# A vision tower with relative attention on one core: the second layer norm's operations dealt out one per head, and four buffers in place of two between the projections and their split

## What is computed

```python
L, H, D, DH, DF = (4, 16, 256, 64, 1024)
h = x                                             # [8, 257, 256]
for i in range(L):
    q, k, val = jnp.split(h @ W_qkv[i], 3, axis=-1)
    q, k, val = (t.reshape(b, s_len, H, DH) for t in (q, k, val))
    kr = (r @ W_r[i]).reshape(s_len, H, DH)
    AC = jnp.einsum('bqhd,bkhd->bhqk', q + u, k)
    BD = jnp.einsum('bqhd,khd->bhqk', q + v, kr)
    prob = jax.nn.softmax((AC + BD) * inv_sqrt_d, axis=-1)
    vec = jnp.einsum('bhqk,bkhd->bqhd', prob, val).reshape(b, s_len, H * DH)
    h = layer_norm(h + vec @ W_o[i], ln1_g[i], ln1_b[i])
    ff = jax.nn.relu(h @ W_ff1[i] + b_ff1[i]) @ W_ff2[i] + b_ff2[i]
    h = layer_norm(ff, ln2_g[i], ln2_b[i])        # the second layer norm
```

## Time and profile before

| what | before |
|---|---|
| median of 3 runs | 2686.0 us (2684.62 to 2693.15) |
| the profiled execution | 2691.76 us, of it 2689.9 us span |
| PE busy | 2219.9 us, 83% of the span |
| DVE busy | 1818.4 us, 68% |
| ACT busy | 1611.9 us, 60% |
| POOL busy | 1186.1 us, 44% |
| head loops (first L1254 of iteration 0 to the last of iteration 31) | 186.6 us to 2349 us of the span, 32 iterations of about 68 us |

### The profile page before, as it was taken

One profiled execution on the slowest core, in us unless ns is written; L12 is line 12 of the kernel. 1 busy time (PEld: TensorE's weight loads), 2 busy tenths in 40 slices (PEclk: granted clock), 3 DMA queues, 4 the chain that ended last, 5 costly groups with the idle time before them and its releaser, 6 DMA issues. The chain is left out here.

```text
span 2689.9 us, 60914 instructions
## 1 busy us (share of the span) xinstructions
PE 2219.9 (83%) x19212; PEld 1640.5 (61%) x19212; DVE 1818.4 (68%) x5490; ACT 1611.9 (60%) x5053; POOL 1186.1 (44%) x2191
## 2 busy tenths in 40 slices
PE   0169989988988988989888898998888999851898
PEld 0146666666666666667666666666666666531565
DVE  8747777777767777777677777776777777625333
ACT  2136666666667666666676666766667667621222
POOL 3025455554555555544565555455655554212011
PEclk9679999999999999999999999999999999975999
DMA  5444333345454333344543333445433333239110
GB/s 166 95 114 105 93 93 93 93 109 140 119 152 103 93 86 93 90 132 125 149 108 93 93 89 93 125 130 142 109 91 91 91 92 90 60 83 311 50 42 26
DMA packets 382056, 285.85 MB, mean 106 GB/s; under 512 B 44711, under 2 KB 350473, under 8 KB 381099
## 3 DMA queue, kind: packets, MB, share of 16 engines
q1 hardware_dynamic: 374603, 262.93, 38.1%
q10 hardware_dynamic: 4864, 12.68, 1.4%
q0 software_dynamic: 2272, 6.35, 0.6%
HBM read 120.84 MB, written 60.48 MB: 67 GB/s over the span
## 5 line engine op out<-in xcount | busy, mean ns | idle before, releaser
L1254 ACT ACTIVATE E<-E,nb 128x257 f32<-128x257 f32 x1024 | 512.8, 508 | 37.1 <-DVE nb L1430 36.9
L975 PE MATMUL bk<-hin,w_sb 128*128 128x257 f16 x3072 | 425.9, 275 | 14.9 <-ACT rel L1192 7.4
L1430 DVE CUSTOM_DVE_ANT_0 E<-bk,cb 128x257 f32<-128x257 f32 x1024 | 390.3, 419 | 64.9 <-PE bk L1068 64.5
L1392 DVE TENSOR_TENSOR pt<-bk,pt 128x512 f16<-128x512 f32 x512 | 354.4, 692 | 64.1 <-ACT pt L1241 55.1
L1023 PE MATMUL bk<-ident,E 128*128 128x128 f32 x2048 | 323.6, 281 | 83.9 <-ACT E L1254 60.5
L975 PEld LDWEIGHTS bk<-hin,w_sb 128*128 128x128 f16 x3072 | 297.1, 98 | 70.0 <-issue 12.6
L1023 PEld LDWEIGHTS bk<-ident,E 128*128 128x128 f32 x2048 | 221.9, 141 | 163.6 <-ACT E L1254 149.8
L1241 ACT ACTIVATE pt<-bk 128x512 f16<-128x512 f32 x512 | 306.4, 598 | 5.8 <-PE bk L1023 5.8
L923 POOL TENSOR_SCALAR wf<-wf 128x256 f32<-128x256 f32 x216 | 93.1, 431 | 434.2 <-DMA wf<-in_w_dram 261.7
L1067 PE MATMUL bk<-kh,qs 128*128 128x257 f16 x1024 | 255.5, 275 | 9.9 <-DMA kl<-rk 9.7
L1068 PE MATMUL bk<-kl,qs 128*128 128x257 f16 x1024 | 255.2, 275 | 0.0
(11 more groups left out here) (277 smaller groups left out, 4409.3 us busy)
## 6 DMA issues: line engine op xcount, KB each, us to landing
qs<-rq SPq DMA_DIRECT2D x256, 128.5 KB, 3.5
kh<-rk SPq DMA_DIRECT2D x256, 128.5 KB, 3.3
kl<-rk SPq DMA_DIRECT2D x256, 128.5 KB, 3.5
wf<-in_w_dram SPq DMA_DIRECT2D x168, 128.0 KB, 2.7
w_split_dram<-wh SPq DMA_DIRECT2D x168, 128.0 KB, 2.2
w_sb<-w_split_dram SPq DMA_DIRECT2D x18, 1024.0 KB, 7.2
wf<-in_we_dram SPq DMA_DIRECT2D x96, 128.0 KB, 2.5
we_split_dram<-wh SPq DMA_DIRECT2D x96, 128.0 KB, 1.8
```

Of the source, the lines that this page charges most:

```text
L975: r = mm(bank[4 + s % 2][:, 0:S], wcol(a, C_QKV, k, 3 * HD, chunk_at(s)), hin[:, m, k, :], start=i == 0, stop=i == 5)
L1254: act.activation(E[:, h % 2, qt, :], E[:, h % 2, qt, :], ACT.Exp, bias=nb[:, 2 * h + qt:2 * h + qt + 1], scale=-1.0, accum_out=sums[:, qt, ...
L1392: v.tensor_tensor(pt[:, h, 1, :, 0:IMG], bank[2 + h % 2][:, :].rearrange("p (k s) -> p k s", k=QT), pt[:, h, 0, :, 0:IMG], ALU.subtract).t ...
L1430: v.tensor_tensor_reduce(E[:, h % 2, qt, :], bank[qt][:, 0:S], cb[:, h, :], -SCORE, 3e38, ALU.add, ALU.min, nb[:, 2 * h + qt:2 * h + qt + ...
```

## The change

The four stages of the second layer norm that worked on both halves (k = 0, 1) in one head take one half per head: normalise in heads 4 and 5, gain in 6 and 7, high part (ScalarE) in 8 and 9, low part in 9 and 10; the copy to `hcls` follows the second low part in head 10. `rel` gets four buffers (`RB_`), slot s goes to buffer s % 4, and `take_q` and `take_k` wait for the split of slot s - 4. The area of on-chip memory reserved for the descriptors of GpSimd's own transfers is set to 8192 bytes a partition (it was left at its default), which makes room for the two buffers. A few waits on constants that GpSimd carried in the gain and the low part are gone.

```diff
+RB_ = 4
-        rel = sb("rel", [P, 2, S])
+        rel = sb("rel", [P, RB_, S])
...
             def split_projection(at, s):
-                pool.tensor_scalar(dst[:, 0, j % NP, :], rel[:, s % 2, :], 1.0, 1.0, ALU.mult, ALU.mult).then_inc(proj_hi, 1)
+                pool.tensor_scalar(dst[:, 0, j % NP, :], rel[:, s % RB_, :], 1.0, 1.0, ALU.mult, ALU.mult).then_inc(proj_hi, 1)
...
-            def ln2_gain(at):
-                for k in range(KC):
-                    n = at.put(count, 2, k - 1)
-                    pool.wait_ge(const_ok, CONST)
-                    pool.wait_ge(scaled2, n)
-                    pool.tensor_scalar(x[:, k, :], x[:, k, :], par[:, G2 + k:G2 + k + 1], par[:, B2 + k:B2 + k + 1],
-                                       ALU.mult, ALU.add).then_inc(z2_ok, 1)
+            def ln2_gain(at, k):
+                pool.wait_ge(scaled2, at(2, k - 1))
+                pool.tensor_scalar(x[:, k, :], x[:, k, :], par[:, G2 + k:G2 + k + 1], par[:, B2 + k:B2 + k + 1],
+                                   ALU.mult, ALU.add).then_inc(z2_ok, 1)
...
+            def ln2_class(at, b):
+                pool.wait_ge(z2_lo, at(2, 0))
                 pool.tensor_copy(hcls[:, :, :, b], hout[:, :, :, CLS]).then_inc(hcls_ok, 1)
...
                 for h in range(H):
                     for s in slots(h, kind):
                         split_projection(at1, s)
-                    if h == 3 and kind.ln2:
-                        ln2_newton(at)
-                    if h == 4 and kind.ln2:
-                        ln2_normalise(at)
-                    if h == 5 and kind.ln2:
-                        ln2_gain(at)
-                    if h == 9 and kind.ln2:
-                        ln2_lo(at, (B if kind.entry else b) - 1)
+                    if kind.ln2:
+                        if h == 3:
+                            ln2_newton(at)
+                        if h in (4, 5):
+                            ln2_normalise(at, h - 4)
+                        if h in (6, 7):
+                            ln2_gain(at, h - 6)
+                        if h in (9, 10):
+                            ln2_lo(at, h - 9)
+                        if h == 10:
+                            ln2_class(at, (B if kind.entry else b) - 1)
...
             def take_q(at, s):
-                if s or not isinstance(at.g, int) or at.g:
-                    act.wait_ge(proj_lo, at(16, s - 1))
+                if at.g or s >= RB_:
+                    act.wait_ge(proj_lo, at(16, s + 1 - RB_))
...
-                    if h == 8 and kind.ln2:
-                        ln2_hi(at)
+                    if h in (8, 9) and kind.ln2:
+                        ln2_hi(at, h - 8)
...
             def take_k(at, s):
-                v.wait_ge(proj_lo, at(16, s - 1))
-                v.tensor_tensor(rel[:, s % 2, :], bank[4 + s % 2][:, 0:S], kr16[:, j - NP, :], ALU.add).then_inc(k_ok, 1)
+                v.wait_ge(proj_lo, at(16, s + 1 - RB_))
+                v.tensor_tensor(rel[:, s % RB_, :], bank[4 + s % 2][:, 0:S], kr16[:, j - NP, :], ALU.add).then_inc(k_ok, 1)
...
-    nc = bacc.Bacc("TRN2", target_bir_lowering=False, num_devices=1)
+    nc = bacc.Bacc("TRN2", target_bir_lowering=False, num_devices=1, dynamic_dma_scratch_size=8192)
```

More of the change, by code:

```diff
@@ L881, in ln2_newton, with ln2_normalise, ln2_lo @@
                 pool.tensor_tensor(y[:, :], y[:, :], t1[:, :], ALU.mult).then_inc(newton2, 1)
-            def ln2_normalise(at):
-                for k in range(KC):
-                    pool.wait_ge(newton2, at(3, 0))
-                    pool.tensor_tensor(x[:, k, :], x[:, k, :], y[:, :], ALU.mult).then_inc(scaled2, 1)
-            def ln2_gain(at):
-                for k in range(KC):
-                    n = at.put(count, 2, k - 1)
-                    pool.wait_ge(const_ok, CONST)
-                    pool.wait_ge(scaled2, n)
-                    pool.tensor_scalar(x[:, k, :], x[:, k, :], par[:, G2 + k:G2 + k + 1], par[:, B2 + k:B2 + k + 1],
-                                       ALU.mult, ALU.add).then_inc(z2_ok, 1)
[L896 to L903, removed]
+            def ln2_normalise(at, k):
+                pool.wait_ge(newton2, at(3, 0))
+                pool.tensor_tensor(x[:, k, :], x[:, k, :], y[:, :], ALU.mult).then_inc(scaled2, 1)
+            def ln2_gain(at, k):
+                pool.wait_ge(scaled2, at(2, k - 1))
+                pool.tensor_scalar(x[:, k, :], x[:, k, :], par[:, G2 + k:G2 + k + 1], par[:, B2 + k:B2 + k + 1],
+                                   ALU.mult, ALU.add).then_inc(z2_ok, 1)
+            def ln2_lo(at, k):
+                pool.wait_ge(z2_hi, at(2, k - 1))
+                pool.tensor_tensor(hout[:, 1, k, :], x[:, k, :], hout[:, 0, k, :], ALU.subtract).then_inc(z2_lo, 1)
+            def ln2_class(at, b):
+                pool.wait_ge(z2_lo, at(2, 0))
                 pool.tensor_copy(hcls[:, :, :, b], hout[:, :, :, CLS]).then_inc(hcls_ok, 1)
@@ L936, in _ @@
                 pool.wait_ge(q_ok, c + 1)
-                pool.tensor_scalar(rq[:, 0, c, :], rel[:, 0, :], 1.0, 1.0, ALU.mult, ALU.mult).then_inc(proj_hi, 2)
+                pool.tensor_scalar(rq[:, 0, c, :], rel[:, s % RB_, :], 1.0, 1.0, ALU.mult, ALU.mult).then_inc(proj_hi, 2)
                 pool.wait_ge(proj_hi, s + 2)
-                pool.tensor_tensor(rq[:, 1, c, :], rel[:, 0, :], rq[:, 0, c, :], ALU.subtract).then_inc(proj_lo, 2)
+                pool.tensor_tensor(rq[:, 1, c, :], rel[:, s % RB_, :], rq[:, 0, c, :], ALU.subtract).then_inc(proj_lo, 2)
             def body(at, l, b, kind):
@@ L958, in _ @@
             ln2_newton(At(pool, L * B))
-            ln2_normalise(At(pool, L * B))
-            ln2_gain(At(pool, L * B))
-            ln2_lo(At(pool, L * B), B - 1)
+            for k in range(KC):
+                ln2_normalise(At(pool, L * B), k)
+            for k in range(KC):
+                ln2_gain(At(pool, L * B), k)
+            for k in range(KC):
+                ln2_lo(At(pool, L * B), k)
+            ln2_class(At(pool, L * B), B - 1)
         @block.tensor
@@ L1209, in first_rstd, with ln2_hi @@
                 act.activation(y[:, :], y[:, :], ACT.Exp, scale=-0.5).then_inc(y_ok, 1)
-            def ln2_hi(at):
+            def ln2_hi(at, k):
                 act.wait_ge(hd_out, at(16, -16))
-                for k in range(KC):
-                    act.wait_ge(z2_ok, at(2, k - 1))
-                    act.activation(hout[:, 0, k, :], x[:, k, :], ACT.Copy).then_inc(z2_hi, 1)
+                act.wait_ge(z2_ok, at(2, k - 1))
+                act.activation(hout[:, 0, k, :], x[:, k, :], ACT.Copy).then_inc(z2_hi, 1)
             def spread_position_term(atl):
@@ L1319, in _ @@
             first_rstd(var2_done, L * B, 7, ln2_ok, y2_ok)
-            ln2_hi(At(act, L * B))
+            for k in range(KC):
+                ln2_hi(At(act, L * B), k)
         @block.vector
```

4 lines of the change are left out of this document (2 added, 2 removed).

## The result

| | median us | runs | ratio to before, 95% interval |
|---|---|---|---|
| before, beside it on the same chip | 2690.6 | 6 | |
| changed kernel | 2676.1 | 6 | 0.9950 [0.9939, 0.9961] |
| changed kernel again, two later jobs | 2673.3 and 2674.5 | 5 and 6 | 0.9946 [0.9932, 0.9959] and 0.9961 [0.9947, 0.9974] |

The forecast was 2676 us and faster by over 0.3%. Both came true, but that 2676 was hit to 0.1 us is luck: the kernel before stood at 2690.6 in this job, 4.6 above the 2686.0 that the forecast started from, and the median fell by 14.5, 4.9 more than the 9.6 of the sum. By the three ratios the change is worth 0.4 to 0.55%, 10.5 to 14.5 us.

The account below looks back on a forecast made before the run. ScalarE was taken to set the head loop's pace, 3.48 us per two heads. Terms -11.0 (ordinary) - 3.5 (closing) - 1.4 + 6.3 (entry) = -9.6 us, from 2686.0 to 2676 us, 0.36% less; range 2667 to 2684.

Parts of the forecast that it names:

- Ordinary loops, 24 x 0.46: Head 7 of 24 ordinary iterations: four buffers remove take_k's 1.11 us wait, 0.46 of it reaching ScalarE; 11.0 us saved.
- Closing loops, -1.2 each: Three closing iterations: TensorE's 0.8 us idle plus head 12's 0.36 come back, 3.5 us in three.
- the same TensorE work can't be done in it in less than 13.2 us: Closing stretch from 675 to 689: TensorE, busy 13.18 of 14.00 us, limits the saving there to 0.8 us.
- point (3): Sign in the closing profile: head 11 about 2.2 us instead of 3.14, heads 7 and 8 together little shorter.
- Entry loops, -1.4 + 6.3: Three entry iterations: head 7 gives back 1.4 us, the class copy 2.1 us later each time costs 6.3.
- The split in one per head, nothing: Layer norm order: gains end 0.8 and 1.0 us before ScalarE's roundings need them, so the move costs nothing.
- The descriptor area, nothing: Expert stage's 17 scatters: some three in flight at a time, so a smaller ring costs nothing.
- rival D: Expert stage: scatters wait for one another in the smaller ring, 29 us slower, 2704 us; chance 0.05.
- Rival B: Closing loops return nothing and ScalarE's separate roundings cost 3.0 us more: no change, 2680 to 2686 us; chance 0.20.
- C: Entry stall caught by later slack, closing loops perhaps giving all 7.4 us: larger gain, 2670 to 2666 us; chance 0.16.
- A: Main case, all loops as worked out: 9.6 us saved, 2676 us; chance 0.54.
- E: Head loops: moved GpSimd instructions collide with VectorE's, 0.48 us each, + 14 us in 30 loops: no change, 2691; chance 0.05.

Follow-up runs that it names:

- only_spread: Changed kernel with two buffers and the default descriptor area, so the new order of one operation per head alone: 2680.5 us, ratio 0.9970.
- early_class: Changed kernel with second low part and class copy ahead of head 10's split on GpSimd: 2676.3 us, 0.9952; run again 2669.8 us, 0.9940.
- late_class: Changed kernel with the second low part and the class copy in head 11 instead of head 10: 2686.2 us, ratio 0.9983.
- only_buffers: Kernel before with the four buffers and the smaller descriptor area, layer norm operations left in their old heads: 2674.6 us, ratio 0.9949.
- late_gain: Changed kernel with the two gains one head later, in heads 7 and 8, ScalarE's roundings where they were: 2691.0 us, ratio 1.0004.
- only_area: Kernel before with nothing but the descriptor area set to 8192 bytes: 2688.9 us, ratio 0.9995.
- after_again: Changed kernel run again without any change, in a later job: 2673.3 us, ratio 0.9946.
- after_third: Changed kernel run a third time without any change: 2674.5 us, ratio 0.9961.
- early_pos9: early_class with the closing loops' position term one head later, in head 9, on TensorE and VectorE: 2670.9 us, 0.9923; run again 2671.1 us, 0.9942.

## Why the prediction was right, point by point

- **Ordinary loops, 24 x 0.46.** 0.47 measured in the same iteration (28.84 to 28.37), -10.4 to -10.9 us in the sum of all 24 by the three traces, each of which has one loop with a late load of `hin`. Right, and with it the way from 1.11 us of VectorE's stall to 0.46 of ScalarE's. What the prediction didn't see is that the new order alone would have done it (only_spread): it priced that part at nothing because it removes no work, but two short stalls cost less than one long.
- **Closing loops, -1.2 each: mis-sized; 1.9 measured**, -5.7 us in three instead of -3.5. The step that was off is "the same TensorE work can't be done in it in less than 13.2 us". TensorE did become the bound, without a gap, but at 12.37 us for 121 instructions that had shown 12.86 busy. Of the 1.98 us that ScalarE gained between heads 7 and 13, 1.31 are TensorE's (0.82 idle and 0.49 hidden in busy time); the other 0.67 is the distance between TensorE's scores and ScalarE's exponentials of head 13, which shrank from 2.04 to 1.37 once VectorE, in between, no longer stood 0.57 at `take_k`. Head 11 came to 1.78, not to the "about 2.2" of point (3): most of ScalarE's transfer starts lie beside other work. Heads 7 and 8 together came to 4.67 from 5.23, 0.56 shorter.
- **Entry loops, -1.4 + 6.3.** The stall of 2.1 us by the replay of GpSimd's queue was measured as 1.93 on TensorE and 2.0 on ScalarE (3.86 against 1.86). early_class shows that the copy is its cause, late_class that there is no slack behind it. The two terms give +1.64 a loop, and a loop in which the clock held is up by 1.55 (0.46 less in head 7, 2.03 more in head 11). But they don't stand on their own: with the copy left in its place the 0.46 is waited away again in head 11 (only_buffers, 32.0), so the buffers are worth nothing here, and the copy's move costs 1.57, not 2.1. What wasn't foreseen is the clock: 1.7 us in each entry where it falls.
- **The split in one per head, nothing.** Right: ScalarE has no new wait for the gain. late_gain shows that the cover of 0.7 to 0.8 us is all there is.
- **The descriptor area, nothing; rival D.** only_area rules D out, for this number of scatters. The waits on constants that GpSimd dropped are gone in only_spread and still there in only_buffers, and the ordinary loops of both are at 28.4.
- **Rival B** is refuted by the closing loops, **C** by the entry loops, though the gain measured lies between A's 9.6 and C's 15.9; the closing loops gave three quarters of C's bound. **E** shows nowhere in the loops: the longest L1394 took 698 ns (L1392 697 before), the longest `take_k` 430 (429 before), and the loops that stick out do so by the late load, which the kernel before has too.
- **The sum.** By the three traces the loops of these kinds sum to -10.91 - 5.73 + 6.88 = -9.76 us (changed), -10.35 - 5.73 + 4.14 = -11.94 (after_again) and -10.48 - 5.72 + 7.40 = -8.80 (after_third). The profiled execution fell by 15.2 us, of which some 5 belong to that one trace of before: against only_area's span the three are 9.6, 12.8 and 12.1 us shorter. The ratios give -10.5 to -14.5, the medians -12.4 to -14.7. What of this lies outside the loops is assigned to nothing: the medians of the kernel before alone lie up to 3.7 us apart.

The best kernel by the traces is the changed one with the class copy ahead of the split: each of its entry loops is at least 1.6 us shorter. With early_pos9, which is one with it in time, it has 0.9939 in the mean of four ratios, against 0.9952 of the changed kernel's three. The medians alone don't settle it: beside the changed kernel it stood 3.0 us above it in one job and 4.7 us under it in the other. With four buffers and the old order (only_buffers) one has nearly the same: the new order then brings next to nothing to the loops (0.1 us in a closing one), and costs the entries 1.6 us each unless the copy is put right.

## What to carry to other kernels

When a stall is to be removed, follow it to the engine that sets the pace and take the difference of that engine's steps, not the stall; then follow that difference to the next wait, for in the entry loops the 0.46 us were taken back four heads later. A moved instruction is charged for what now stands ahead of the one result that another engine waits for in order: two instructions set ahead of a low part and a copy of 0.2 us cost 4.7 us in three places, most of the 5.7 that the closing loops brought, and 1.7 more wherever the clock fell. And work that looks movable because nobody in the loop waits for it may feed a store and a load whose reader is in the next stage; look there for the price before splitting it.

## What the hardware showed that was not expected

- TensorE's clock sometimes fell after it had stood 1.9 us at its wait: in 5 of the 15 entries of the five traces with that wait (changed, after_again, after_third, only_spread, late_gain), in none of 15 where the wait was 0.25 to 0.35 us (only_buffers, early_class and early_pos9 twice each), and in all three of late_class after 3.04 us. The twelve products then take 4.04 to 4.44 us instead of 2.75. The price of a short wait on TensorE is thus not fixed: 1.9 or 3.6 us. What decides it from one entry to the next isn't shown.
- TensorE's busy time isn't a floor for its work: 121 instructions were busy 12.86 us with waits between them and 12.37 without. Each visible pause hid 0.16 us more, the part of the last matmul (0.27 us) that the next one (0.11 behind it) would have overlapped.
